# Attention tower on one core: norm moments on GpSimd, levels in halves, states by head, score products of one tile in one mixed block, a new order of work

## What is computed

```python
h = einsum('bfh,kh->bfk', frames(x), D)                     # DCT
a = layernorm(h); n = layernorm(a)*g + b                    # 1: attention
xq, xk, xv, xg = mixes of n with n shifted by one token
q, k = exp(rmsnorm(xq @ Wq.T)), exp(rmsnorm(xk @ Wk.T)); v = xv @ Wv.T
A_t = lam * A_{t-1} + k_t v_t^T;  z_t = lam * z_{t-1} + k_t # per head, decays over k's index
att = sigmoid(xg @ Wg.T) * (q_t^T A_t) / (q_t . z_t) @ Wo.T
a = a + att; a = a + gelu(layernorm(a) @ W1.T) @ W2.T
h = h + a
m = layernorm(h); xa = layernorm(m) @ Wat.T + b + m         # 2: expert of the sequence
y = gelu(xa @ fc1.T + b1) @ fc2.T + b2
out = h + gelu(y @ Wnext.T + bn)
```

## Time and profile before

| | |
|---|---|
| median of 3 runs | 1221.79 us (1215.12 to 1226.37) |
| the profiled execution | 1218.9 us, its span 1217.1 us |
| PE, DVE, ACT, POOL busy | 94%, 81%, 51%, 25% of the span |
| TensorE's granted clock | 0.99 of full |

### The profile page before, as it was taken

How to read it: one execution, slowest core, us unless ns; L and a number is a source line. 1 busy time by engine, 2 the same in 40 slices (tenths; PEclk the granted TensorE clock), 3 DMA queues, 4 the chain that set the end, 5 groups by cost and what they waited for, 6 DMA issues and landing times.

```text
span 1217.1 us, 43497 instructions
## 1 busy us (share of the span) xinstructions
PE 1138.9 (94%) x17955; PEld 807.8 (66%) x17955; DVE 986.5 (81%) x3362; ACT 621.5 (51%) x1100; POOL 300.9 (25%) x174
## 2 busy tenths in 40 slices
PE   4799999999999999999999999999999999999997
PEld 4576676666767676766666667666676766667664
DVE  7878788797887979788796887979879797987962
ACT  3346446363554736446363554736446364554634
POOL 4123131221403223131311403223131221403211
PEclk8799999999999999999999999999999999999999
DMA  5321313222141312313222141312313222141210
GB/s 188 106 64 39 113 43 110 65 79 56 43 132 44 87 47 66 110 43 113 63 78 55 44 130 46 88 45 63 112 44 110 63 80 57 43 132 45 87 55 17
DMA packets 51492, 91.48 MB, mean 75 GB/s; under 512 B 9536, under 2 KB 26592, under 8 KB 51296
## 3 DMA queue, kind: packets, MB, share of 16 engines
q1 hardware_dynamic: 51296, 88.69, 24.1%
HBM read 19.50 MB, written 9.78 MB: 24 GB/s over the span
## 4 chain that ended last, share of the span: by engine, by line
PE 83%; DVE 9%; POOL 4%; issue 3%; ACT 2%; DVEq 0%; POOLq 0%
PE bank L1056 10%; PE bank L1049 9%; PE bank L1084 9%; PE bank L1078 8%; PE bank L919 8%; PE bank L914 7%; PE bank L1014 7%; PE bank L998 5%; PE bank L990 4%; PE bank L1033 4%; POOL nrm L391 3%; PE bank L1029 3%; PE bank L954 3%; PE bank L943 2%; PE bank L994 2%
## 5 line engine op out<-in xcount | busy, mean ns | idle before, releaser
L514 ACT ACTIVATE px<-bank 128x512 f32<-128x512 f32 (+1 forms) x128 | 72.8, 569 | 218.0 <-PE bank L998 152.9
L763 DVE COPY_PREDICATED px<-mask,bank 128x512 f32<-128x512 uint32 (+1 forms) x128 | 88.6, 692 | 79.6 <-issue 76.8
L1078 PE MATMUL bank<-xa,f1w 128*128 128x512 f32 (+1 forms) x256 | 124.7, 587 | 14.8 <-DVE qtok L704 13.0
L1056 PE MATMUL bank<-w,hid 128*128 128x128 f32 x1024 | 121.9, 277 | 17.2 <-ACT hid L533 17.2
L1056 PEld LDWEIGHTS bank<-w,hid 128*128 128x128 f32 x1024 | 116.7, 192 | 31.6 <-ACT hid L533 31.6
L1014 PEld LDWEIGHTS bank<-qx,ki 128*32 128x32 f32 x7680 | 89.6, 110 | 42.3 <-issue 33.9
L827 DVE TENSOR_TENSOR ki<-k,rp 128x96 f32<-128x96 f32 (+13 forms) x512 | 113.2, 295 | 0.6 <-ACT k L499 0.6
L397 POOL TENSOR_TENSOR ab<-af,heads 128x896 f32<-128x896 f32 x16 | 40.8, 2552 | 291.1 <-DVE af L755 291.1
L1049 PE MATMUL bank<-c,w 128*128 128x512 f32 (+1 forms) x256 | 111.4, 568 | 1.1 <-ACT c L527 0.9
L1084 PE MATMUL bank<-hid,f2w 128*128 128x512 f32 (+1 forms) x256 | 107.5, 563 | 0.0
L1014 PE MATMUL bank<-qx,ki 128*32 128x16 f32 x7680 | 99.2, 193 | 6.9 <-issue 6.6
(11 more groups left out here) (142 smaller groups left out, 2414.0 us busy)
## 6 DMA issues: line engine op xcount, KB each, us to landing
qx<-qq SPq DMA_DIRECT2D x256, 96.0 KB
hs<-hs SPq DMA_DIRECT2D x32, 532.0 KB, 4.4
v<-v_f SPq DMA_DIRECT2D x16, 512.0 KB, 3.9
gz<-gate_f SPq DMA_DIRECT2D x16, 512.0 KB, 4.7
xT<-in_xT SPq DMA_DIRECT2D x16, 468.5 KB, 4.0
f1w<-in_fc1T SPq DMA_DIRECT2D x16, 256.0 KB, 2.7
f2w<-g_dram SPq DMA_DIRECT2D x16, 256.0 KB, 3.0
out<-t_sum SPq DMA_DIRECT2D x16, 256.0 KB, 2.7
```

What stands on the lines that cost most here:

```text
L763: V.copy_predicated(px[c % 2][0:n, :, 0:n], mask[0:n, 0:n].rearrange("p (o m) -> p o m", o=1).to_broadcast([n, HEADS, n]), bank[DIAG][0:n, ...
L1056: last = mm(dst[:, P * i:P * i + P], hid[:, j, P * m:P * m + P], w2[:, j, :], start=(j == 0), stop=(j == 3))
L1078: mm(dst[:, 0:width[g]], f1w[:, P * j:P * j + P], xa[:, cols(g)], start=True, stop=True).then_inc(f1_ok, 1)
```

## The change

1. The moments (mean and variance out of bn_stats' six numbers) move from DVE to POOL: six small operations (moments) and one or two more before each power, with a wait between dependent ones. gathered, DVE's twice_normed and variance1 go.
2. qlev, inside and between work on a half (512 tokens) at once: half as many instructions over the same elements. klevels now waits (last_pairs) for the tiles of the other half.
3. states and ab go. scan takes the entering state by head: four 32x32 products from af in place of one of 128x128.
4. pairs_a and pairs_b become one function pairs(b, c). The 64-key product becomes two of 32 keys, and the order inside a tile mixes long products of windows 0 and 1 with short ones of 3 and 2. pairs(b, c) starts only when both banks of tile c - 1 have been read (pxa_ok and px_ok).
5. All five orders and USES are new. In PE's round, stage 0 now holds only the DCT and the first transposes of a sequence, and what is left of a sequence goes one round further (LAST = 3).

The core of the diff:

```diff
+            def moments(st, mv, sums, odd, s, up, n):
+                gp.tensor_tensor(sums[:, s, :], st[:, s, 1:3], st[:, s, 4:6], ALU.add)
+                gp.tensor_tensor(odd[:, s], st[:, s, 1], st[:, s, 4], ALU.subtract).then_inc(up, 1)
+                gp.wait_ge(up, n + 1)
+                gp.tensor_tensor(odd[:, s], odd[:, s], odd[:, s], ALU.mult)
+                gp.tensor_scalar(mv[:, s, 0], sums[:, s, 0], 0.5, None, ALU.mult).then_inc(up, 1)
+                gp.wait_ge(up, n + 2)
+                gp.tensor_scalar(odd[:, s], odd[:, s], 32.0, None, ALU.mult).then_inc(up, 1)
+                gp.wait_ge(up, n + 3)
+                gp.tensor_tensor(odd[:, s], odd[:, s], sums[:, s, 1], ALU.add).then_inc(up, 1)
+                gp.wait_ge(up, n + 4)
             def pow3(b, g):
-                gp.wait_ge(var3, nth(b, 2, g + 1))
+                gp.wait_ge(bn3, nth(b, 2, g + 1))
+                before(gp, n2_ok, b, 2, g + 1)
+                moments(st3, mv3, sm3, od3, four(g), mo3, nth(b, 10, 5 * g))
+                twice_normed(vv3, od3, four(g), mo3, nth(b, 10, 5 * g + 5))
...
-                    w = scan_w[g] if m <= WIN else GRP
+                    w = HALF if m > WIN else min(HALF, WINS * WIN - HALF * g)
...
+            def pairs(b, c):
...
+                if n == NW:
+                    other_half(0)
+                    other_half(1)
+                    next_window(2)
+                    for j in range(EIGHT):
+                        own_block(3, j)
+                        own_block(2, j)
+                next_window(0)
+                for j in range(1, NE):
+                    for w in range(n - 1, -1, -1):
+                        last = later_block(w, j)
+                last.then_inc(pa_ok, 1)
                 for j in range(EIGHT):
+                    own_block(1, j)
+                    last = own_block(0, j)
                 last.then_inc(pb_ok, 1)
...
                 if c:
-                    mm(S[:, s0:s0 + n], ab[:, c - 1, :], qc[:, P * c:P * c + n], start=True, stop=False, skip_group_check=True)
+                    for hd in range(HEADS):
+                        r = slice(HD * hd, HD * hd + HD)
+                        mm(S[r, s0:s0 + n], af[r, c - 1:HD * NST:NST], qc[r, P * c:P * c + n], start=True, stop=False, skip_group_check=True)
...
-LAST = 2
+LAST = 3
```

More of the change, by code:

```diff
@@ L359, in body @@
                 if (b := at(1)) is not None:
[L360 to L366 removed]
+                    hand_h1(b); spread(b, 1); hand_v(b)
             every_round(body)
@@ L838, in body @@
             def body(at):
+                if (b := at(1)) is not None:
+                    mixes(b, 1); sums(b, 0, 0); sums(b, 0, 1); mixes(b, 2)
+                if (b := at(2)) is not None:
+                    normed3(b, 0)
+                if (b := at(1)) is not None:
+                    sums(b, 1, 0); norms(b, 0); sums(b, 1, 1); tokens(b, 0, 0); tokens(b, 0, 1); mixes(b, 3)
+                if (b := at(2)) is not None:
+                    hidden(b, 1)
+                if (b := at(1)) is not None:
+                    norms(b, 1); tokens(b, 1, 0); tokens(b, 1, 1); qlev(b, 0)
+                if (b := at(2)) is not None:
+                    x_attn(b, 0)
+                if (b := at(1)) is not None:
+                    between(b, 0); inside(b, 0)
+                if (b := at(2)) is not None:
+                    stats3(b, 1)
+                if (b := at(1)) is not None:
+                    from_start(b); decayed(b); merge(b, 0)
+                if (b := at(2)) is not None:
+                    normed3(b, 1)
+                if (b := at(1)) is not None:
+                    zscan(b); merge(b, 1); chain(b); zmul(b); merge(b, 2); qlev(b, 1); inside(b, 1); denominators(b)
+                    merge(b, 3); between(b, 1); gate(b, 0); gate(b, 1)
+                if (b := at(2)) is not None:
+                    x_attn(b, 1)
+                if (b := at(1)) is not None:
+                    merge(b, 4); gated(b, 0); merge(b, 5); attended(b, 0); stats2(b, 0)
                 if (b := at(0)) is not None:
@@ L857, in body @@
                 if (b := at(1)) is not None:
[L858 to L883 removed]
+                    normed2(b, 1); hidden(b, 0); stats3(b, 0)
             every_round(body)
@@ L1093, in body @@
+                if (b := at(1)) is not None:
+                    pairs(b, 0)
+                if (b := at(2)) is not None:
+                    f2s(b, 0)
+                if (b := at(1)) is not None:
+                    pairs(b, 1); us(b)
+                if (b := at(2)) is not None:
+                    nmTs(b, 1); n1Ts(b, 1)
+                if (b := at(1)) is not None:
+                    scan(b, 0); pairs(b, 2); scan(b, 1)
                 if (b := at(0)) is not None:
-                    dcts(b, 0); dcts(b, 1)
+                    dcts(b, 0)
@@ L1095, in body @@
                 if (b := at(1)) is not None:
-                    pairs_b(b, 7); n2Ts(b, 0); scan(b, 6); scan(b, 7); w1s(b, 0, 0); w1s(b, 0, 1); attends(b, 1)
+                    pairs(b, 3); gates(b, 1); zts(b); scan(b, 2)
+                if (b := at(0)) is not None:
+                    dcts(b, 1)
+                if (b := at(1)) is not None:
+                    scan(b, 3); rTs(b, 0); rTs(b, 1)
+                if (b := at(2)) is not None:
+                    ats(b, 1)
+                if (b := at(1)) is not None:
+                    pairs(b, 4)
@@ new lines, in body @@
+                if (b := at(2)) is not None:
+                    f1s(b, 1, 0); f1s(b, 1, 1); f1s(b, 1, 2)
+                if (b := at(1)) is not None:
+                    pairs(b, 5); attends(b, 0)
+                if (b := at(2)) is not None:
+                    f1s(b, 1, 3)
+                if (b := at(1)) is not None:
+                    scan(b, 4)
+                if (b := at(2)) is not None:
+                    oTs(b, 0)
+                if (b := at(1)) is not None:
+                    pairs(b, 6)
```

376 lines of the change are left out of this document (164 added, 212 removed), and 10 rows, old and new, of the table USES.

## The result

The kernel after takes 1274.82 us (median of 4 runs, 1272.23 to 1277.08), the kernel before 1219.97 in the same runs: ratio 1.0446, 95% interval 1.0391 to 1.0501. It is slower by 55 us; forecast were 1191 us and a range up to 1228.

The account below looks back on a forecast made before the run. PE, busy 94% of the span, was taken to bound the kernel. Ramp, 13 rounds of 70.6 us and tail (5.5 + 56 + 68 + 13 x 70.6 + 140) gave a span of 1187, hence 1191 us; range 1163 to 1228.

Parts of the forecast that it names:

- POOL's small operations: Seven or eight small operations added to each of five chains on POOL: 0.2 us each, bounds 0.11 and 0.37.
- The latency of a norm: Moments chain on POOL: 2.0 us against some 0.6 on DVE, bounds 1.2 and 3.4, plus waiting for two-input DVE operations.
- The walk through the round: Step-by-step count from the end of transposes nTs(b, 1): scores start at 25.3 us, round 70.6 us, 2.4 less.
- under 2 as the sign: Expected in the profile after: normed3's first operation on DVE waits for POOL under 2 us a round.
- 1.5 + 0 + 0.9: Waits for powers in a round: 1.5 us before normed3(b, 0), none for x, 0.9 on PE around normed3(b, 1).
- The tile: Full tile of scores on PE: 1.67 us against 1.80 to 1.9, seven a round, 1.6 us a round saved.
- States by head: Entering state on PE as four products on 32 rows and columns: +0.2 us a round, ends -1.5 and +1.0.
- DVE's work: Aggregates leave and 32 fewer level instructions: DVE falls from 60.6 to some 55 us a round, about 880 in all.
- The ramp and the tail: First two spacings of DCTs 56 and 68 us; behind the last DCT 140 us in place of 117.
- power latency in place of the old waits: Rival: POOL operations cost 0.37 us and each chain loses one mix; round 73.0, 1222 us, no change; chance 0.20.
- the chain of 5 us by the full rule: If each small POOL operation could lose a DVE mix of 1.1 us, a moments chain could take 5 us.
- long products that hold up short ones: Rival: score products start strictly in order on PE; tile 2.2 us, round 74.3, 1243 us; decides from 1.95; chance 0.10.

Follow-up runs that it names:

- a_dve: The kernel after with all three sets of moments back on VectorE, GpSimd keeping the powers: 1221.1 us, ratio 0.9993 to the kernel before.

## Why the prediction was wrong, step by step

- **POOL's small operations**: 0.2 us chosen, 0.20 to 0.24 measured, and a free chain as forecast: x's first half takes 3.01 us from statistics to power. Right.
- **The latency of a norm**: the mechanism is as forecast, a POOL operation that arrives during a two-input operation waits for its end. Where the text worked a chain out, its size was nearly right too: for h1's first it gave 4.8 to 5.5 us from the statistics to the power (5.7 to 10.5 or 11.2), and 5.75 were measured. A chain is seven or eight small operations and the power; what the held ones took beyond 0.20 makes 1.8 to 1.9 us of each, and without it they would be 3.0 (x) and 3.9 us (h1).
- **The walk through the round** is the step that failed: the waits for the powers were left out or taken too small. x's second half was given none, though its chain runs beside the shift and the first mix: 4.79 us, a wait of 1.21 on DVE and 1.16 on PE. By that all behind it comes later. Counted from the end of the transposes nTs(b, 1), the statistics of h1 end at 7.0 us for 5.7, the power is ready at 12.7 for 10.5 to 11.2, and DVE waits 2.39 us for the 1.5 taken. For h1's second chain 0.9 was taken for PE; DVE waits 3.06, PE 0.78 and 0.70 here and 1.0 in the mean, so this term was near. The scores start at 29.2 us and not at 25.3. Of these 3.9 us the powers make 2.1; most of the rest is in DVE's own list, where one small norm of 8 columns beside a residual sum of POOL takes 1.12 us. PE is idle 4.9 us a round for the 2.7 of the sum, and DVE waits 5.45 us a round for h1's powers where the text named under 2 as the sign. a_dve, without the chains, has rounds of 72.58 us: on POOL they cost 3.6 us a round, where 1.5 + 0 + 0.9 had been put down.
- **The clock** was no term at all. In the kernel after it costs little. Once PE is the bound it costs 9 us for each 0.010, and a_dve with the 0.990 of the profiled kernel before would take some 18 us less by this count, an estimate of 1203. The four rounds of a_dve at the full clock took 69.9 to 70.7 us, about the 70.6 of the forecast, but that is partly luck: the forecast had 2.4 us in it for chains that a_dve doesn't have. PE's work in these rounds is 69.3 us for the 68.6 forecast.
- **The tile**: 1.67 forecast, 1.71 measured, against 1.87 before, for a wrong reason. The text put the gain on products that run beside each other; it is all in the split of the 64-key product. That mode was in the rows before, and no term priced it.
- **States by head**: +0.2 a round forecast, about +0.4 measured, and no matter.
- **DVE's work**: 55 us a round forecast, 55.75 measured (911.5 us in all for 880, which left out the ramp and the tail). Right, and worthless: the time saved there became waiting time.
- **The ramp and the tail**: 59.3, 73.6 and 146.7 us for 56, 68 and 140, 16 us of the 88 by which the span was missed; the other 72 are 13 rounds of 76.15 for 70.6.
- **Rivals**: the first, power latency in place of the old waits, is what happened, at 76.2 us a round for the 73.0 that it was given, because it too has nothing for x's wait and no term for the clock. Its chance of 0.20 and its time of 1222 us were both too low; the chain of 5 us by the full rule, which the text names, is near what came. The second, long products that hold up short ones, stays out: in the kernel after a tile never took 1.95 us but for half clock and waits. By the rule of the Trainium skill that it cited (TensorE: Matmul & The Clock Gate, section The mechanism) it worked out 2.2 us for a tile; the trace does not agree: it shows 1.71, and the product behind the two long ones starts 0.23 us ahead of their second records (605.25 and 605.48).

## What to carry to other kernels

Before small dependent operations go to GpSimd, list what VectorE runs in the time they have, and allow for each that can begin inside a two-input or a long one-input operation the rest of it, or of a whole run of them. Walk through every chain, also the one that seems short: a wait left out early shifts all that follows. Here the chains whose consumer is near lost more than VectorE gained, and the one with slack (the first normalisation) was free. Then look at the granted clock of each variant beside its time: what a new order saves on TensorE can be lost there. And try to split a product whose mode differs from that of its neighbours before reordering them.

## What the runs showed of the hardware that was not expected

- A GpSimd operation of 128x4 was held for 4.96 us, across nine two-input VectorE instructions in a row.
- One-input operations of VectorE over 896 to 1024 columns (0.62 to 0.71 us) hold GpSimd as well: 0.53 to 1.10 us for 0.20. Statistics, reductions and copy_predicated never did (0.19 to 0.25 us beside them).
- The granted clock fell to its lower level for 3.4 us with PE busy 7.60 of the 7.90 us before, and with one unread product of 0.9 us a round ahead of that place 34 us less stood at half speed (0.970 to 0.984).
- One product in 64-column mode among products of 32 columns costs 0.26 us more than two of 32 (1.97 and 1.70 us a tile).
